# An attention stage on one core: which probability tiles the accumulating transfers sum, and which TensorE sums

## What is computed

```python
logits = jnp.einsum('bhik,bhjk->bhij', q, k)
a = jax.nn.softmax(logits, axis=-1)
y = jnp.einsum('bhij,bhjv->bhiv', a, v)
```

## Time and profile before

| | |
|---|---|
| median of 3 runs | 3648.7 us (3648.08 to 3656.93) |
| profiled execution | 3653.45 us |
| its span, first to last instruction | 3651.7 us, mean granted clock 0.973 |
| PE busy in the span | 3451.7 us (95%) |
| POOL busy | 2095.9 us (57%) |
| DVE busy | 2051.3 us (56%) |
| ACT busy | 1515.4 us (41%) |
| DMA queue 0 (issued by GpSimd) | 23.7% of 16 engines |
| DMA queue 1 (issued by SyncE) | 25.9% of 16 engines |

### The profile page before, as it was taken

How to read it: one execution, slowest core, us unless ns; L and a number is a source line. 1 busy time by engine, 2 the same in 40 slices (tenths; PEclk the granted TensorE clock), 3 DMA queues, 4 the chain that set the end, 5 groups by cost and what they waited for, 6 DMA issues and landing times. The chain is left out here.

```text
span 3651.7 us, 47181 instructions
## 1 busy us (share of the span) xinstructions
PE 3451.7 (95%) x16672; PEld 2252.2 (62%) x16672; DVE 2051.3 (56%) x3299; ACT 1515.4 (41%) x2791; POOL 2095.9 (57%) x1663
## 2 busy tenths in 40 slices
PE   7999899999999999999999969999999986999997
PEld 5777445454554545455455348888888864777776
DVE  5776677777777777777777244222222213444443
ACT  2332366666666666666666622111111112211121
POOL 3654388887878888798888712222222213545453
PEclk9999899999999999999999979999999997999999
DMA  4555676868677786877765543222222114212221
GB/s 170 183 172 196 119 145 126 154 132 146 132 139 151 127 145 131 153 140 132 151 128 107 105 149 97 65 63 74 74 71 68 57 41 143 80 59 82 75 75 38
DMA packets 176739, 419.34 MB, mean 115 GB/s; under 512 B 15382, under 2 KB 62998, under 8 KB 151670
## 3 DMA queue, kind: packets, MB, share of 16 engines
q1 hardware_dynamic: 153606, 249.59, 25.9%
q0 software_dynamic: 22896, 166.73, 23.7%
HBM read 162.25 MB, written 87.03 MB: 68 GB/s over the span
## 5 line engine op out<-in xcount | busy, mean ns | idle before, releaser
L845 DVE TENSOR_REDUCE part_max<-ps_att 128x1 f32<-128x512 f32 x1972 | 1227.9, 684 | 400.3 <-PE ps_att L763 399.9
L891 ACT ACTIVATE probs<-ps_att 128x512 f32<-128x512 f32 x2048 | 1062.4, 602 | 545.1 <-PE ps_att L735 469.8
L942 POOL TENSOR_TENSOR prob_sums<-prob_sums,probs 128x512 f32<-128x512 f32 x884 | 1146.9, 1562 | 61.8 <-DMA probs<-probs 61.8
L787 PE MATMUL ps_att<-probs,v_tok 128*32 128x512 f32 x4096 | 550.7, 610 | 0.0
L1433 POOL TENSOR_TENSOR ff_g_lo<-ff_g,ff_g_hi 128x512 fp32r<-128x512 f32 x128 | 165.1, 1290 | 551.6 <-DVE ff_g_hi L1394 551.6
L735 PE MATMUL ps_att<-q_stack,k_first 97*128 97x512 f32 x768 | 328.0, 427 | 14.1 <-ACT probs L891 14.0
L735 PE MATMUL ps_att<-q_stack,k_stack 97*128 97x512 f32 x768 | 321.4, 427 | 10.6 <-ACT probs L891 10.0
L1302 ACT ACTIVATE ff_g<-ps_ff 128x512 f32<-128x512 f32 x128 | 76.8, 600 | 579.6 <-PE ps_ff L1186 579.6
L763 PE MATMUL ps_att<-k_first,q_stack 96*128 96x512 f32 x756 | 304.6, 403 | 7.3 <-DMA q_stack<-qk 7.3
L763 PE MATMUL ps_att<-k_stack,q_stack 96*128 96x512 f32 x768 | 303.7, 395 | 0.0
L735 PEld LDWEIGHTS ps_att<-q_stack,k_first 97*128 97x128 f32 x768 | 146.5, 191 | 199.4 <-ACT probs L891 141.3
(11 more groups left out here) (202 smaller groups left out, 5705.0 us busy)
## 6 DMA issues: line engine op xcount, KB each, us to landing
probs<-probs POOLq DMA_DIRECT2D x159, 1024.0 KB, 8.7
q_stack<-qk SPq DMA_DIRECT2D x144, 128.0 KB, 7.2
qk<-rot_hi SPq DMA_DIRECT2D x64, 256.0 KB, 6.5
qk<-rot_lo SPq DMA_DIRECT2D x64, 256.0 KB, 2.4
av_gate_rows<-gate SPq DMA_DIRECT2D x64, 256.0 KB
k_stack<-qk SPq DMA_DIRECT2D x24, 512.0 KB, 11.0
k_first<-qk SPq DMA_DIRECT2D x18, 512.0 KB, 10.8
x_in_sb<-in_x SPq DMA_DIRECT2D x8, 1024.0 KB, 6.7
```

The lines of the kernel that those rows point to most:

```text
L787: mm = nc.tensor.matmul(o_ps[rows, :], t["v"][:, steps[w]["b"], k, rows], t["p"][:, w % PR, h, :], start=(k == 0), stop=(k == LT - 1))
L845: nc.vector.tensor_reduce(t["pm"][:, r, k:k + 1], mx[mx_uses % 3], AX.X, ALU.max)\
L891: nc.scalar.activation(t["p"][:, at % PR, h, :], sT[(at * G + h) % 3], ACT.Exp)\
L942: nc.gpsimd.tensor_tensor(x, first, t["p"][:, w % PR, h, :], ALU.add).then_inc(s["acc_done"], 1)
```

## The change

The tables that share out the 16 tiles of a block are others. Before, TensorE sums tiles 8 and 14; five pairs (0,1), (3,4), (6,7), (9,10), (12,13) are summed by transfers; tiles 2, 5, 11 and 15 are added singly. After, TensorE sums tile 15; six pairs (0,1), (2,3), (5,6), (8,9), (10,11), (13,14) are summed by transfers; tiles 4, 7 and 12 are added singly. The rounds stay eight to a block. `last_sums` moves from step 5 to step 7 of the next block. TensorE's first sum of a block, which opens the bank `l_ps`, is now tile 15, and its wait for the bank (`l_kept`) stands there. The first round waits for tile 4's exponentials too. Block 31 has six sums on TensorE before and after.

```diff
--- before.py
+++ after.py
@@ -32,16 +32,16 @@
 EPS2 = 1e-6
 EPS_ATT = 1e-30
 PR = 8
-PE_SUMS = (8, 14)
-PAIRS = (0, 3, 6, 9, 12)
-POOL_FIRST = 2
-POOL_ROUNDS = ((5, 0), (7, 5), (9, 3), (11, 6), (12, 11), (14, 9), (16, 15), (18, 12))
+PE_SUMS = (15,)
+PAIRS = (0, 2, 5, 8, 10, 13)
+POOL_FIRST = 4
+POOL_ROUNDS = ((5, 0), (7, 2), (9, 7), (11, 5), (13, 8), (15, 10), (17, 12), (19, 13))
 POOL_ADDS = G * len(POOL_ROUNDS)
-LAST_SUMS = (8, 11, 12, 13, 14, 15)
+LAST_SUMS = (10, 11, 12, 13, 14, 15)
 LAST_ROUNDS = tuple(x for x in POOL_ROUNDS if x[1] not in LAST_SUMS)
 K_AT = (2, 6, 10, 14, 18, 22)
 V_AT = (26, 30)
-LAST_AT = 5
+LAST_AT = 7
 STEPS = NB * LT
 UNITS = NG * B
 JOBS = G * TT
@@ -791,12 +791,13 @@
             def sums(w):
 
                 n, k = w // LT, w % LT
-                if k == PE_SUMS[0] and n:
+                opening = k == shares(n)[0][0]
+                if opening and n:
                     pe.wait_ge(s["l_kept"], n)
                 pe.wait_ge(s["exp"], G * (w + 1))
                 for h in range(G):
                     mm = nc.tensor.matmul(l_ps[h * KD:(h + 1) * KD, :], c["ones"][:, 0:KD], t["p"][:, w % PR, h, :],
-                                          start=(k == PE_SUMS[0]), stop=False)
+                                          start=opening, stop=False)
                 mm.then_inc(s["psum"], 1)
 
             def last_sums(n):
@@ -935,6 +936,7 @@
                     if r == 0:
                         if n >= 2:
                             pool.wait_ge(s["sum_done"], n - 1)
+                        pool.wait_ge(s["exp"], (n * LT + POOL_FIRST) * G + h + 1)
                         first = t["p"][:, POOL_FIRST % PR, h, :]
                     else:
                         pool.wait_ge(s["acc_done"], n * POOL_ADDS + G * (r - 1) + h + 1)
```

## The result

| | before | after |
|---|---|---|
| median | 3648.4 us (3647.9 to 3656.9, 4 runs) | 3677.8 us (3673.9 to 3683.9, 4 runs) |
| ratio | | 1.0064, 95% interval 1.0045 to 1.0083 |
| profiled execution, span | 3653.45, 3651.7 us | 3683.88, 3682.1 us |

The change makes the kernel slower, by 0.64% in the ratio on record (some 23 us); the medians above are 29 us apart. Repeated on another chip the ratio was 1.0060 (1.0042 to 1.0078). The kernel before had a median of 3648 us on the first chip and of 3654 to 3657 on the others, so the experiments are compared by their ratio to it and not by their times.

A forecast was written before the change was run, and what follows sets the result against it. TensorE's sequence was taken as the bound, with late transfers at second blocks of units. -26.7 us (removed sum) + 32 (boundaries) = +5 on 3653.45, 3658.7; the median runs 4.75 lower, so 3654 us, range 3619 to 3689.

The forecast's parts named there:

- the third, DMA-bound and slower: Unit boundaries: first pairs of the next block late too, clock falls every time, 14 us each, 3689 us; chance 0.29.
- the fourth: Every block's start: the maxima's copies come 1.3 us late in 31 blocks, +40 us, 3694 us; chance 0.06.
- the signs named: Undisturbed blocks 50.8 us, second blocks 58 to 62, GpSimd idle 5 or more, lower clock, additions wait near 130, 190 transfers.
- The sum that goes: TensorE loses one tile's sum in blocks 0 to 30, 0.86 us each on the path: -26.7 us.
- GpSimd's own work at nothing: GpSimd in undisturbed blocks: busy 45.1 us instead of 44.5, below TensorE's 50.8, so no cost.
- The DMA engines full in the first two blocks of a unit: Two more transfers make 102.3 us of DMA work where TensorE wants 101.6, so the engines must be late.
- The late place is again the round of the last pair: Second blocks of units: the last pair's transfer lands late behind the q load, 9 us per boundary, 63 in all, +32.
- the light ones: Second blocks that lost 2.2 us before; their last transfer now falls behind the whole q load, 8.9 us each.
- the count of 31 us: What seven second blocks of units (1, 5, 9, 13, 17, 21, 25) lost above 51.7 us before the change.
- The price of the lower clock: TensorE after long gaps: heavy blocks lost 2.5 to 4 us, of which 1.5 was taken for the clock.
- Pair 12's transfer moves behind the copies: At the maxima's copies: the transfer that lay across them before moves behind them, the argument against late copies.
- rival 2: DMA queues: pair transfers and q loads share engines evenly, so boundaries cost 15 us or less, 3606 us; chance 0.10.

The follow-up runs named there:

- e2_spread: The changed kernel with the next unit's k and v loads spread over the unit's four blocks; ratio to before 0.9837, median 3594.9 us.
- e3_before_spread: The kernel before the change with the next unit's k and v loads spread over the unit's four blocks; ratio to before 0.9894, median 3615.9 us.
- e4_five: The changed kernel without pair (13,14)'s transfer: tile 13 added singly by GpSimd, tile 14 summed by TensorE; ratio to before 0.9928, 3630.8 us.
- e12_ahead_k15: The changed kernel with the maxima one step further ahead and the fourth k load at step 15 instead of 14; ratio to before 1.0028.
- e10_after_k13: The changed kernel with the fourth k load of a unit at step 13 instead of 14; ratio to before 1.0008.
- e8_no10: The changed kernel without pair (10,11)'s transfer: tile 10 added singly, tile 11 summed by TensorE; ratio to before 0.9985.
- e1_ahead: The changed kernel with the maxima one step further ahead (AHEAD 20 instead of 19), which also moved a k load earlier; ratio to before 0.9998.

## Why the prediction was right and wrong

The time, 3677.8 us, lies in the range of 3619 to 3689, but the likeliest case, 3654 us and no change that can be told, did not come. Of the rivals the third, DMA-bound and slower, comes nearest in time (3689), with the lower clock at every boundary as it said, and a part of the fourth inside it. That its number fits is in part luck: it put 14 us on each second block, and what was measured is 6.7 on the first and 6.5 on the second. Of the signs named, 50.8 us, 190 transfers and the lower clock came; ScalarE's wait for additions was 93.2 us and not near 130, and in block 9 GpSimd stood idle 1.62 us for the last pair and not 5.

- **The sum that goes: right.** Undisturbed blocks are 50.8 us, as written. Over the whole stage it is 22.5 us by e2_spread and e3_before_spread, 25.1 without block 0, where 26.7 was forecast.
- **GpSimd's own work at nothing: right.** It is busy for 45.55 us of 50.8 in block 10, and TensorE is busy for the whole block.
- **The DMA engines full in the first two blocks of a unit: right as a count**, and the loads there are the cause, as e2_spread and e3_before_spread show. 102.3 us of work were counted for two blocks; blocks 8 and 9 took 114.1 us, at shares of 0.98 and 0.91, and with the loads spread they took 101.6. The step from full to late ("they can't be full now without being late") is not shown: with the loads spread, two blocks at 0.92 and 0.96 are not late, and those of e4_five at 0.93 and 0.88 are hardly so (51.8 and 52.2 us against 51.7).
- **"The late place is again the round of the last pair", and its price: wrong, the step that failed.** The boundary's cost was reckoned from the last pair alone, 2.3 us more for each second block and a jump of 2.9 for the light ones, 9 us each, 63 in all. What became late was the chain behind it: GpSimd waited 6.72 and 3.22 us for pairs 0 and 2 of the unit's first block, pair 8 went out 7.3 us later than in an undisturbed block, and pair 10 slid from 6.1 us in front of the maxima's copies onto them. The first block of each unit, undisturbed before (51.7), became 57.5 us, which no term of the sum held; second blocks rose only from 56.0 to 57.3. Above 50.8 the disturbed blocks cost 6.7 + 6.5 = 13 us a unit and not 9. Over units 0 to 6, without block 0, that is 83 us where 63 was forecast, and 20 of the 25 us between the forecast for the profiled execution and its time; most of the rest is the 7.6 us behind the stage. (Block 0 was disturbed before the change already, 58.4 us, which the count of 31 us left out; it is 56.6 after.) The walk through the block had been made in an undisturbed block only.
- **The price of the lower clock: too small.** "2.5 to 4 us in the steps after the gap" was read too narrowly: from the earlier trace rows, what blocks 1, 9 and 17 lost above 51.7 us while TensorE was busy is 3.8, 4.7 and 1.9 us. The sum took 1.5 us more for each of four second blocks, 6 in all; the estimate above is 24 us in units 1 to 6, since the clock fell 12 times there, in the first block and the second of each unit.
- **"Pair 12's transfer moves behind the copies", against rival 4: wrong where it mattered.** It holds in undisturbed blocks. Its price, 40 us if in 31 blocks, was 34.8 us in 14, and by e12_ahead_k15 and e10_after_k13 some 4 to 13 us were to be had by taking it away.
- **The even share of the queues (rival 2): no support.** Pair 13's transfer was issued at 888.13, 1.4 us behind the q load, and GpSimd began its round at 903.94, 15.8 us later. It was not tested by itself.

## What to carry to other kernels

If several queues feed on the same DMA engines, add up their work over the fullest stretch, not over the whole run; the shares of 24% and 26% of the span said nothing of 0.89 in block 8, nor of 0.98 there with one more transfer. Then look at what meets what in that stretch: one load moved by one step was worth 0.73% with the same bytes. Before trading engine time for transfers, spread the prefetches: that took two lines, was worth 1.06% by itself, and turned the change from a loss of 0.64% into a gain of 0.57% of the kernel before. And in an experiment that moves one thing, run the control on the kernel before: here it showed that a queue which issues in order had moved a second thing along. Compare times of two executions from the start of the block, since by then one of them is ahead.

## What was not expected of the hardware

Four copies of 2 KB, which let TensorE go on 5.5 us after the first is issued in undisturbed blocks, took 9.4 us in block 8, where a 1 MB transfer was issued 0.5 us after the first of them and the DMA engines were at 0.98. Without that transfer, in e8_no10, TensorE never waited for them. Behind a gap of only 2.69 us in TensorE's work, which ended at 890.62, the granted clock fell; the stretch behind it:

```profile
892.50:896.00 3.50, 3.50 (x17) 1.35 (x19) 2.07 (x3) 1.50 (x3) 3.50 (x3) 0.50 0.96 125
```

There it is 0.50, the level of 1.2 GHz. In e1_ahead no gap of units 1 to 6 was longer than 1.3 us, and it never fell there. And two kernels with the same packets and bytes in both queues, e4_five and e8_no10, are 0.57% apart.
